# Four layers on one core: exponents by matmul, delayed squares, moved size sums

## What is computed

```
x = _layernorm(x + _L0_attn_ref(x, ...))   # stage A: up, gate, Taylor terms, SwiGLU of 1248
x = _layernorm(x + _L0_ffn_ref(x, ...))    # stage B: SwiGLU of 1376 with LoRA of rank 16
x = _layernorm(x + _L1_attn_ref(x, ...))   # stage C: Mamba2, 128 heads of 64, state 128, chunks of 128
x = _layernorm(x + _L1_ffn_ref(x, ...))    # stage D: SwiGLU of 2048 with ternary weights
```

```
seg = cs[..., :, None] - cs[..., None, :]
Lmat = jnp.where(tri, jnp.exp(seg), 0.0)
scores = jnp.einsum('bclhn,bcshn->bchls', Cc, Bc) * Lmat
Ydiag = jnp.einsum('bchls,bcshp->bclhp', scores, xdt)
...
yg = y * jax.nn.silu(gate)
rstd = jax.lax.rsqrt(jnp.mean(jnp.square(yg_g), axis=-1, keepdims=True) + EPS)
```

## Time and profile before

| | |
|---|---|
| median of 3 runs | 2425.5 us (2418.97 to 2426.75) |
| the profiled execution | 2427.0 us, its span 2424.3 us |
| PE busy | 2160.4 us (89%), granted clock 0.957 |
| DVE busy | 1969.4 us (81%) |
| ACT busy | 1176.2 us (49%) |
| POOL busy | 864.5 us (36%) |
| stage A, to its last residual sum | about 277 us |
| stage B | about 265 us |
| stage C | about 1,660 us, of it the 64 units about 1,490 |
| stage D | about 220 us |

### The profile page before, as it was taken

How to read it: one execution, slowest core, us unless ns; L and a number is a source line. 1 busy time by engine, 2 the same in 40 slices (tenths; PEclk the granted TensorE clock), 3 DMA queues, 4 the chain that set the end, 5 groups by cost and what they waited for, 6 DMA issues and landing times. The chain is left out here.

```text
span 2424.3 us, 36666 instructions
## 1 busy us (share of the span) xinstructions
PE 2160.4 (89%) x10833; PEld 1709.6 (71%) x10833; DVE 1969.4 (81%) x2969; ACT 1176.2 (49%) x2125; POOL 864.5 (36%) x478
## 2 busy tenths in 40 slices
PE   7898679979979999999999999999999999975987
PEld 5676568767867777777777777777777777754865
DVE  5444354547869999999999999999999999987887
ACT  2322211114356666666666666666656666641222
POOL 5425033421124444435335435435335435430000
PEclk9999889999989999999999999999999999987988
DMA  5414130003231221221212212122121221202433
GB/s 192 153 56 143 46 134 0 0 24 85 82 118 50 61 80 44 66 66 56 66 57 66 65 57 66 44 78 61 48 78 44 66 78 44 70 0 92 143 113 107
DMA packets 125940, 175.66 MB, mean 72 GB/s; under 512 B 17668, under 2 KB 83716, under 8 KB 125316
## 3 DMA queue, kind: packets, MB, share of 16 engines
q1 hardware_dynamic: 125892, 175.07, 22.8%
HBM read 165.72 MB, written 9.31 MB: 72 GB/s over the span
## 5 line engine op out<-in xcount | busy, mean ns | idle before, releaser
L70 PE MATMUL bank<-xT_hi,C_w_hi 128*128 128x512 f32 x1160 | 479.4, 413 | 16.0 <-POOL C_w_lo L1360 7.6
L71 PE MATMUL bank<-xT_lo,C_w_hi 128*128 128x512 f32 x1160 | 466.2, 402 | 0.0
L72 PE MATMUL bank<-xT_hi,C_w_lo 128*128 128x512 f32 x1160 | 465.7, 401 | 0.0
L1360 POOL TENSOR_TENSOR C_w_lo<-C_raw,C_w_hi 128x512 fp32r<-128x512 f32 x130 | 207.6, 1597 | 493.0 <-ACT C_w_hi L1465 328.8
L1237 DVE TENSOR_SCALAR C_decay<-C_cs_second,C_cs_t 128x128 f32<-128x128 f32 x512 | 324.0, 702 | 2.6 <-DMA C_cs_second<-cs_rows 2.6
L1119 DVE SCALAR_TENSOR_TENSOR C_acc<-bank,C_par,C_acc 128x510 f32<-128x510 f32 (+2 forms) x384 | 281.0, 744 | 46.5 <-ACT C_acc L1425 23.7
L1225 DVE TENSOR_TENSOR C_decay<-C_decay,C_cb 128x512 f32<-128x512 f32 x384 | 290.7, 783 | 2.5 <-ACT C_decay L1551 2.5
L70 PEld LDWEIGHTS bank<-xT_hi,C_w_hi 128*128 128x128 f32 x1160 | 223.4, 193 | 75.3 <-POOL C_w_lo L1360 8.9
L72 PEld LDWEIGHTS bank<-xT_hi,C_w_lo 128*128 128x128 f32 x1160 | 222.7, 192 | 54.7
L71 PEld LDWEIGHTS bank<-xT_lo,C_w_hi 128*128 128x128 f32 x1160 | 223.6, 193 | 48.2
L1379 POOL TENSOR_TENSOR C_sg<-C_xs 128x1024 f32<-128x1024 f32 x56 | 127.8, 2281 | 303.4 <-DVE C_xs L1200 303.4
(11 more groups left out here) (246 smaller groups left out, 4468.1 us busy)
## 6 DMA issues: line engine op xcount, KB each, us to landing
C_raw<-in_Cxg SPq DMA_DIRECT2D x65, 512.0 KB, 3.6
C_cs_second<-cs_rows SPq DMA_DIRECT2D x64, 512.0 KB, 4.9
C_raw_out<-in_Cout SPq DMA_DIRECT2D x64, 256.0 KB, 3.5
D_raw<-in_D SPq DMA_DIRECT2D x32, 512.0 KB, 3.6
A_raw<-in_A SPq DMA_DIRECT2D x20, 512.0 KB, 5.4
A_stat_raw<-in_D SPq DMA_DIRECT2D x16, 512.0 KB, 3.5
D_raw<-in_D SPq DMA_DIRECT2D x32, 256.0 KB, 2.6
cb_rows<-C_decay SPq DMA_DIRECT2D x8, 768.0 KB, 3.3
```

The lines of the kernel that those rows point to most:

```text
L70: pe.matmul(out, lh, rh, start=start, stop=False)
L71: pe.matmul(out, lh, rl, start=False, stop=False)
L72: return pe.matmul(out, ll, rh, start=False, stop=stop)
L1360: e.tensor_tensor(w_lo[:, slot, :], raw_at, f32(w_hi[:, slot, :]), ALU.subtract).then_inc(lo_done, 1)
```

## The change

In stage C the second chunk's cs[l] - cs[s] is now made like the first chunk's, by matmuls from rows that hold the bf16 parts of cs and the mask. `left`, `right` and the parts get a dimension for the chunk, `chunk_rows` holds both, `load_rows` issues four transfers instead of two. `seg(u, c)` does both heads of chunk c; the second call stands behind `in_g` and waits until ScalarE has read the first chunk's exponents out of the same banks. The clamps are gone; the exponents of the second chunk read the banks and not SBUF. Since masked exponents are now 0 in both chunks, `move_cb` copies without a mask, in three instructions instead of five. The order on ScalarE is first chunk, across, second chunk.

GpSimd's `squares` in a unit's body waits besides for all six rounds of that unit. `squares_sum` moves from the end of a group's first unit to between the halves of `in_x` of its second, `mean_square` to behind the first half's convolution, `root` behind the two silu.

The size tiles move from stage A to B: two in each of the last three tiles of the first half, one in each of the first ten of the second half. Their buffer lies over `right_raw`, which is free once `packed` is 7.

```diff
             if kind == "B":
...
+                sp.wait_ge(packed, 7)
+                for i in range(D_TILES):
+                    if i >= 2:
+                        sp.wait_ge(abs_done, 3 * (i - 1))
+                    sp.dma_start(stat_raw[:, i % 2, 0:2 * D], extra["D13"][i, :, :]).then_inc(stat_in[i % 2], 16)
+                    sp.dma_start(stat_raw[:, i % 2, 2 * D:3 * D], extra["D2"][i, :, :]).then_inc(stat_in[i % 2], 16)
                 return
...
+        def size_tiles(hf, n, par):
+
+            if hf == 0:
+                if isinstance(n, int) and n >= STAT_FROM:
+                    return [(2 * (n - STAT_FROM) + j, j) for j in range(2)]
+                return []
+            return [] if isinstance(n, int) and n + STAT_EARLY >= D_TILES else [(n + STAT_EARLY, par)]
...
             def squares(u):
...
                 e.wait_ge(S.gated, u.V * 2 + 2)
+                if u is not last:
+                    e.wait_ge(S.m_done, u.U * ROUNDS + ROUNDS)
...
-                clamp(u, 0)
-                clamp(u, 1)
...
+                if u.group_ended:
+                    root(u.g)
                 if not u.first:
                     y_high(u, 0)
-                decay_exp(u)
+                inside_exp(u, 0)
+                across_exp(u)
+                inside_exp(u, 1)
...
+                for h in range(2):
+                    if c:
+                        pe.wait_ge(S.decays, u.U * EXPS + (h + 1))
+                    elif not u.first:
+                        pe.wait_ge(S.xd_done, u.V * 2 + (h + 1))
+                    pe.matmul(bank[6 + h][:, :], left[:, c, h, :], right[:, c, h, :], start=True, stop=False)
...
             def body(u):
                 in_x(u, 0)
+                if u.group_ended:
+                    squares_sum(u)
                 in_x(u, 1)
...
                 seg(u, 0)
-                seg(u, 1)
                 in_g(u, 0)
                 in_g(u, 1)
+                seg(u, 1)
...
                 turn(u, 0)
                 turn(u, 1)
-                if u.group_ends:
-                    squares_sum(u)
```

More of the change, by code:

```diff
@@ L579, in body @@
                              .then_inc(term_ready, 1)
-                    if kind == "A" and not (isinstance(n, int) and n >= D_TILES // 2):
-                        i = n + hf * (D_TILES // 2)
+                    for i, slot in size_tiles(hf, n, par) if kind == "B" else ():
                         v.wait_ge(abs_done, i * 3 + 3)
-                        if hf == 0 and isinstance(n, int) and n == 0:
+                        if isinstance(i, int) and i == 0:
                             v.tensor_copy(sh.abs_totals[:, :], stat_sum[:, 0, :]).then_inc(stat_added, 1)
@@ L586, in body @@
                             v.wait_ge(stat_added, i)
-                            v.tensor_tensor(sh.abs_totals[:, :], sh.abs_totals[:, :], stat_sum[:, par, :], ALU.add)\
+                            v.tensor_tensor(sh.abs_totals[:, :], sh.abs_totals[:, :], stat_sum[:, slot, :], ALU.add)\
                              .then_inc(stat_added, 1)
@@ L977, in state_space @@
         dtz, dta, dte = quarters[0:3]
-        ends, ends_rest = quarters[3][:, 0:HALF], quarters[3][:, HALF:N]
+        ends = quarters[3][:, 0:HALF]
         dts, cs, reset = sq_sum, sg[:, 0, :], sg[:, 1, :]
@@ L1225, in decay_round @@
                 v.tensor_tensor(e, e, cb[:, r % 2 if r < 4 else 2, :], ALU.mult).then_inc(S.m_done, 1)
-            def clamp(u, h):
-                if h == 0:
-                    v.wait_ge(cs_in[u.j], (u.U - u.j) * 8 + 16)
-                    wait(v, S.y_mm, u.U * 2)
-                    if u.first:
-                        v.wait_ge(S.cb_stored0, 8 * GROUPS)
-                        v.wait_ge(S.cb_stored1, 8 * GROUPS)
-                for b in range(BATCH):
-                    t = slice(P * b, P * (b + 1))
-                    v.tensor_scalar(decay[:, 4 + h, t], cs_second[:, u.j, HALF * h + P * b:HALF * h + P * (b + 1)],
-                                    cs_t[:, 2 * b + 1, bass.ds(u.U * 2 + h, 1)], 0.0, ALU.subtract, ALU.min)\
-                     .then_inc(S.clamped, 1)
             def x_steps(u, h):
@@ L1310, in body @@
                         conv(v, bank[h], lambda n: par_of(U, n), acc[:, :], h, i, S.conv, U * 6)
+                    if u.group_ended and h == 0:
+                        mean_square(u, g)
                 if not u.first:
@@ L1532, in gate_silu, with inside_exp, across_exp @@
                 a.activation(sg[:, u.j, half(h)], bank[2 + h][:, :], ACT.Silu).then_inc(S.g_silu, 1)
-            def decay_exp(u):
+            def inside_exp(u, c):
+                for h in range(2):
+                    if c == h == 0:
+                        wait(a, S.y_mm, u.U * 2)
+                        if u.first:
+                            a.wait_ge(S.cb_stored0, 8 * GROUPS)
+                            a.wait_ge(S.cb_stored1, 8 * GROUPS)
+                    a.wait_ge(S.seg_mm, u.U * 4 + (2 * c + h + 1))
+                    to = decay[:, 4 + h, :].rearrange("p (b l) -> p b l", b=BATCH) if c else \
+                        decay[:, 2 * h:2 * h + 2, :].rearrange("p r (b c l) -> p (r b) c l", b=2, c=2)[:, :, 0, :]
+                    a.activation(to, bank[6 + h][:, :].rearrange("p (b l) -> p b l", b=BATCH), ACT.Exp).then_inc(S.decays, 1)
+            def across_exp(u):
                 for h in range(2):
@@ L1611, in cb_blocks @@
                 pe.wait_ge(S.bc_silu, 4 * g + 4)
-                wait(pe, S.cb_moved, 5 * g)
+                wait(pe, S.cb_moved, 3 * g)
                 if g == 0:
```

144 lines of the change are left out of this document (59 added, 85 removed).

## The result

The changed kernel runs at **2456.5 us** (2454.99 to 2458.67, 4 runs) against 2424.2 (4 runs): ratio **1.0143**, 95% interval 1.0131 to 1.0156. It is slower by 1.4%, where 2434 was forecast with a range up to 2456. The side was right, the size was not: +32 instead of +10, and the time lies just above the range.

A forecast was written before the change was run, and what follows sets the result against it. VectorE, busy 179.18 of 185.16 us per group, was taken as the bound, with a loop through GpSimd next. Terms -22 + 32 - 1.5 + 0 + 1.5 - 3 = +7 on 2427.0 gave 2434 us, range 2388 to 2456.

The forecast's parts named there:

- stage A: SP's queue no longer waits for ScalarE's size sums before loading weights, so TensorE waits less: -22 us (-12 to -29).
- start of stage C: Four row transfers instead of two before the first sum, doubled steps on cs parts, more masks: +1.5 us (0 to +5).
- seven groups: Stage C: a group of eight units takes 190.6 us against 186.0 in the mean, +4.6 seven times: +32 us.
- end of stage C: The last inside products waited 6.45 us for VectorE and would now wait 3.4: -3 us.
- The loop squares, low part, gate products: Each unit: delayed squares make the gate weights' low part late, TensorE waits 0.8 us; unit 22.3 us against 22.49.
- The 5.4 us before squares_sum: A group's second unit: TensorE idles for the delayed squares before squares_sum, forecast as 5.6 us.
- The third unit's wait behind GpSimd's clearing: A group's third unit: output weights' low part comes after group sums and clearing; tiles wait 4.3 us, unit 26.3.
- rounds with all operands in SBUF are held by GpSimd: VectorE's decay round takes 1.18 us instead of about 0.68 beside GpSimd; without such holding the sum is 25 us lower.
- Holding grows: Rival: output weights' low parts delay exponents and rounds by 0.5 us in every second unit; 2450 to 2465 us, chance 0.14.
- the eight one-column products: A group's second unit, after the squares_sum wait: 1.8 us for these, +1.6 for slow clock behind; unit 30.5.
- up to 1.6 of slow clock, 0.5 taken: A group's third unit: slow TensorE clock on the tiles after their wait, 0.5 us counted in its 26.3.
- the forecast's 22.3: Plain unit of stage C: 21.5 us of TensorE work, new sums included, plus a 0.8 us wait for gate weights.

The follow-up runs named there:

- experiment 1: The kernel before with only the size tiles moved from stage A to B, clamps and old stage C kept: 2405.1 us, ratio 0.9936.
- experiment 3: The changed kernel with GpSimd's low parts of gate and output weights ahead of the delayed squares: 2425.5 us, ratio 1.0015.
- experiment 4: The changed kernel with squares_sum moved to just before the gate products, in bank 3: 2385.9 us, ratio 0.9862.
- experiment 8: The changed kernel with the squares waiting for four of the six rounds: 2450.3 us, ratio 1.0115.
- experiment 9: Experiment 2 with, in GpSimd's even units, the output weights' low part behind that of the x weights: 2347.6 us, ratio 0.9694.
- experiment 12: The kernel before with size tiles in B, clamps kept, squares delayed, low parts ahead of squares, squares_sum just before the gate products: 2314.3 us, ratio 0.9549.
- experiment 2: The changed kernel without the squares' wait for the rounds: 2364.3 us, ratio 0.9773.
- experiment 5: The changed kernel with the edits of experiment 3 and experiment 4 together, delay kept: 2350.6 us, ratio 0.9729.

## Why the prediction was right or wrong

Both profiled executions, by the ends of the stages and the starts of TensorE's units:

| term | forecast | measured |
|---|---|---|
| stage A | -22 | -21.1 |
| stage B | 0 | -0.9 |
| start of stage C | +1.5 | +1.6 |
| first group | -1.5 | -0.5 |
| seven groups | +32 | +48.6 |
| end of stage C | -3 | +2.4 |
| stage D | 0 | -1.6 |
| sum | +7 | +28.5 |

*Right, and shown:* stage A (experiment 1). The loop squares, low part, gate products: experiment 3 takes the low part out of it, and the wait goes; the price of a plain unit was 0.2 too high. The 5.4 us before squares_sum: experiment 4. The third unit's wait behind GpSimd's clearing: its row, though at 2.52 it is under the 3 to 5 that were to show it. That rounds with all operands in SBUF are held by GpSimd: experiment 8, whose theory of unheld rounds gave 2375 where 2450 was measured. The Trainium skill ("Advanced Engine Details and Errata", VectorE Performance Modes, Mode Summary) names only two-port modes and GpSimd as blocking each other; by that alone the rounds would not be held, and these rows speak against it. "Holding grows" has the measured time in its range of 2450 to 2465, but by chance: its mechanism would have made every second unit longer, and the plain units are 22.1. Without the delay it does happen (experiment 9).

*Wrong:* the step "the eight one-column products then take 1.8, and nine products behind them 3.7 instead of 2.1, so +1.6: the clock is granted at its 1.2 GHz level after 2.4". It carried the prices of a 1.57 us stop over to one of 5.6. The granted clock of that row was not read: it is 1.00 over the 1.81 us and 0.54 only behind it. In the changed kernel the sums took 3.43 and the stretch behind them 1.8 too long. The second unit came to 32.9 instead of 30.5, which is 2.4 x 7 = 17 of the 21 missing us. Of these, up to 10 could have been seen beforehand: the row was one group's end out of seven, and three of the others lose 3.1 us to the clock and not 1.6.

In the same way the third unit's "up to 1.6 of slow clock, 0.5 taken" measured 1.4 to 2.8, 2.1 in the mean. It came to 27.1 and not 26.3, 0.8 x 7 = 6 more; that it was not 11 is luck, as its stops were 0.8 shorter than forecast. Plain units gave 8 back, and the groups of before were 2 us shorter in all than the mean I had taken.

*Left out:* what follows at stage C's end, +2.4 instead of -3. The step "now it is 3.4: -3" is right for the inside products (3.19 of waiting, TensorE's row at 2180.37), but behind them the last low parts of the output weights stand in GpSimd's queue after the squares. The first tile comes 13.06 us behind the last transposes, where it was 12.95 before: nothing is gained. GpSimd's timeline there, changed kernel:

```profile
2180.40 2.33 POOL L1369 TENSOR_TENSOR C_sg<-C_xs 128x1024 f32<-128x1024 f32 x1 [14.81 <-DVE C_decay L1228]
2182.81 2.35 POOL L1372 TENSOR_TENSOR C_sq_sum<-C_sq_sum,C_sg 128x1024 f32<-128x1024 f32 x1
2185.12 1.72 POOL L1348 TENSOR_TENSOR C_w_lo<-C_raw,C_w_hi 128x512 fp32r<-128x512 f32 x1
2186.80 3.38 POOL L1356 TENSOR_TENSOR C_out_lo<-C_raw_out,C_out_hi 128x512 fp32r<-128x512 f32 x2
```

TensorE, its first tile behind the inside products:

```profile
2190.24 0.79 PE L70 MATMUL bank<-C_out_hi,C_yg_hi 128*128 128x512 f32 x1 [5.36 <-POOL C_out_lo L1356]
```

The other 2.1 are the clock again. Windows view of the stretch from the first tile to the last sums, before and then after:

```profile
2162.43:2173.44 11.01, 11.01 (x48) 9.09 (x49) 4.85 (x5) 1.28 (x1) 4.38 (x2) 1.00 0.01 1
...
2190.24:2203.38 13.14, 13.14 (x49) 10.64 (x50) 3.26 (x5) 0.00 (x0) 4.61 (x2) 0.83 0.00 0
```

*Not said:* the forecast's 22.3 had the new sums in "21.5 us of TensorE work", without seeing that on a closed loop they count in full while VectorE's gain counts nothing. The delay alone costs 17 us, the new exponents beside it another 35, though by themselves they gain 41; the forecast had one mechanism for both and no price for the two together.

Not tried: the clamps with the reordered queues and no delay, which would tell whether experiment 12 needs the delay; the kernel without the delay and with both low parts of the output weights over the convolution sums; and any way to move GpSimd's clearing, which is the third unit's last wait (2.1 us in experiment 12). The split of a stop's price into waiting and clock rests on rows of the traces; no run changed the clock alone, and why the same stop costs more in one group than in the next is open.

## What to carry to other kernels

Work that is held by a neighbour engine may be cheaper to move apart than to replace: the clamps took 5.4 us beside GpSimd's squares and 1.65 elsewhere; replacing them gave 41 us (2405 to 2364, with squares_sum moved, which is worth 2 of it at most), moving the squares away, with the queues on both sides reordered, 91 (2405 to 2314), and both together only 55 (to 2350.6), since the matmuls then add TensorE's work where TensorE is the bound. When a wait is added in front of an instruction, take what is queued behind it out of the way first, on its own queue and on the reader's; here two reorderings were worth 106 us. And price a stop of TensorE by the granted clock on both sides of it, at every place where such a stop occurs and not at one: here one length had two prices, and a longer one a third.

## What was not expected of the hardware

- A stop's price in clock is not given by its length. After 1.53 to 1.57 us the kernel before lost 1.5 us in four groups and 3.1 in three. After 2.52 to 2.54 the tiles of experiment 4 took 5.57 in one group and 6.9 to 7.2 in six, those of the changed kernel up to 8.4. Only after 5.38 and 6.47 (experiment 3) was the 1.2 GHz level there from the first sum on in all seven groups; after 5.38 the sums and the products behind them took 8.5 us instead of 5.0 (experiment 2, from 2.88 to 7.85 into the unit).
- The clock can fall behind a stop of hardly any length: in experiment 5, two of seven groups had a second unit of 25.4 instead of 23.8, after a wait of 0.28 us and the eight one-column sums.
- Half a delay was dearer per unit than a whole one: 23.3 against 22.1, and 22.2 with none. The cost of GpSimd's 4.8 us depends on which of VectorE's instructions lie beside it: rounds and y_low are held (0.68 became 2.00, 0.74 became 1.76), convolution sums and out_adds, which read PSUM, are not.
